# Attention outputs turned by DMA and divided on VectorE, and three smaller edits, in a one-core decoder layer

## The chip, the cores and the metric

One core of a Trainium2 chip runs the whole kernel. The metric is device time in microseconds (us). The kernel before was timed three times: 1709.32 us median, 1707.47 to 1713.86. Engines: PE is TensorE (matmuls and transposes by matmul), PEld its weight loads, DVE is VectorE, ACT is ScalarE, POOL is GpSimd, SP is SyncE, which here only starts DMAs.

## The reference, cut to what matters

Eight batches of 512 queries and 256 dims attend to 1601 context rows, with 16 heads of 16 dims. A self-attention before it touches only 16 rows per batch, and the feed-forward network after it picks one of eight adapters per batch.

```python
x = _layernorm(x + self_attention(x))                    # its result changes 16 rows per batch
q, k, v = split_heads(x @ Wq.T), split_heads(mem @ Wk.T), split_heads(mem @ Wv.T)
scores  = einsum('bhqd,bhkd->bhqk', q, k) / sqrt(16)     # 8 x 16 x 512 x 1601
out     = einsum('bhqk,bhkd->bhqd', softmax(scores), v)
x = _layernorm(x + merge_heads(out) @ Wo.T)
top1 = argmin over the 8 units of mean((decode(encode(x)) - x)**2)
x = _layernorm(x + x @ W_base + b_base + adapter[top1](x))
```

## The kernel before, in words

**Tiling.** Cross-attention is done in 32 groups (8 batches x 4), a group being 4 of the 16 heads. A group is 13 slots, one for each tile of 128 context rows. So a batch is 52 slots (numbered 0 to 51 below) and the kernel 416. In every slot (`pe_slot`) PE makes four score tiles [128 keys x 512 queries], one for each head, from stacked bf16 parts (`pe_scores`). ACT turns each into probabilities (`act_exp`), and PE multiplies those of the slot before with the values (`pe_values`). `values` is one PSUM bank in which each head has 32 partitions: 16 rows of unnormed output and one row of sums of exponentials.

**Maxima.** The exponentials need each query's maximum. Two slots' worth of work ahead, PE makes the scores a second time, queries by keys (`pe_pair`, two double-bank tiles per slot), and DVE reduces each of them (`dve_pair`). In slot 9 of a group DVE joins the pieces and splits the maxima into two bf16 parts (`dve_max_parts`). PE then turns them (job `max`), DVE copies them out of PSUM, ACT's queue writes them to DRAM and reads them back as two more rows of the query stack (`act_max_out`, `act_max_in`), so that the score matmul subtracts them.

**Jobs.** All else goes through one PSUM bank, `work` (`W`): two tables written by hand say which job stands in the middle of a slot (`IN_BETWEEN`) and which at its end (`SLOT_END`). A job has the bank alone; the semaphores `work_full` and `work_free` count through them. A group's output is such a chain: ACT copies `values` to `oS` (`xo_unnormed`) in the next group's first slot (`act_values_out`); job `otr` turns it on PE in four transposes (L932); DVE takes reciprocals of the sums and multiplies into `ox` (L1434, L1435). Once for a batch, jobs `oT` turn `ox` back (2 x 4 transposes, ACT copies each), and jobs `xo` multiply with Wo. DVE's other small work stands in `VECTOR_WORK`, by slot.

**SP's queue.** `sp_batch` is a fixed order of DMA issues, each behind the semaphores that it needs; SP waits at each. `sp_stacks` builds half a batch's stacks: 6 query DMAs, 6 key DMAs, 2 mask DMAs ("top"), then 6 and 6 more ("low").

**PSUM.** `banks` has six banks: two for scores (`SRING`), and two tiles of two for the maxima (`MRING`). The last group has no maxima to make ahead. After it `pe_tail` finishes the last batch.

Of the kernel before, what the change touches and what calls it, by code (L numbers as in the profile page):

```python
# [23 lines left out]
P = 128  # L24
# [6 lines left out]
GH = 4  # L31
# [59 lines left out]
def program(nc, g):  # L91

    with ExitStack() as whole:
# [21 lines left out]
        g.max_dram = nc.dram_tensor("max_dram", (2 * GH * QT, P), BF16, kind="Internal").ap()  # L115

# [29 lines left out]
def short_self_attention(nc, g, s, view, beside):  # L146
# [38 lines left out]
    adiff = sb("s_abs_diff", [TOK, D])  # L185
# [527 lines left out]
def cross_attention_and_ffn(nc, g):  # L713

    sem, W, ident, ident_b, scores, pairs, av = g.sem, g.W, g.ident, g.ident_b, g.scores, g.max_scores, g.av
    Wb = W[:].bitcast(BF16)
    with ExitStack() as s:
# [43 lines left out]
        ox = sb("ox", [P, QT, D])  # L761
# [3 lines left out]
        err = sb("err", [P, 2, T])  # L765
        loss = sb("loss", [P, NPAIR])
# [15 lines left out]
        evac = sem("x_values_out")  # L782
        x1_in = sem("x_x1_in")
# [4 lines left out]
        own = {e: sem(f"x_own_{e}") for e in ("dve", "pool")}  # L788

        def signals(stage):  # L790
# [106 lines left out]
        def work_in_order():  # L897

            for sl in range(B * SLOTS):
                job, part, parts = at_end(sl)  # L900
                for one in (in_between(sl), job if part == 0 else None):
                    if one:
# [10 lines left out]
                         20: ("kproj", 7, 0), 22: ("v", 6, 0), 24: ("qproj", 1, 0), MXG + 1: ("max", 0, 0),  # L913
                         MXG + 2: ("v", 7, 0), MXG + 4: ("v", 0, 0), MXG + 6: ("v", 1, 0)}
# [35 lines left out]
        def pe_job(ph, job, part=0, parts=1):  # L950
# [21 lines left out]
            elif name == "oT":  # L972
                last = transposes(W, ox, i)
# [114 lines left out]
        def pe_next_pair(of, x):  # L1088
# [1201 lines left out]
```

## Time and profile before

| | |
|---|---|
| median of 3 runs | 1709.32 us |
| the profiled execution's own time, as its span | 1708.3 us |
| PE busy | 1623.0 us (95%) |
| DVE busy | 1234.7 us (72%) |
| ACT busy | 1063.1 us (62%) |
| mean granted TensorE clock | 0.991 |
| DMA queue of SP, share of 16 engines' span | 33.7% |

The span runs from the first to the last instruction of the profiled execution. Busy shares are means over stages that differ: the main loop is about 1530 us of it, from the first slot at 122.8 us. A slot's length can be read from the timeline as the distance between two starts of its first pair of score matmuls (L1107).

### The profile page before, as it was taken

Reading aid. Unit: us, or ns where it says so; the run is one execution under the profiler, and the core shown is the slowest. Engines: PE = TensorE matmul, PEld = TensorE weight load, DVE = VectorE, ACT = ScalarE, POOL = GpSimd, SP = SyncE. Lnnn points to the kernel's source line nnn. Section 1 sums busy time; section 2 is a strip of 40 time slices with the busy share of each in tenths; the row PEclk is TensorE's granted clock in tenths of the full one; section 3 lists DMA queues with packets and bytes.
Section 4 is the critical chain, followed back from the end, with each engine's and each line's share of the span. In section 5 each row is a group of like instructions: output and inputs, shape, how many; then the busy total and the mean of one; then the engine's idle time right before and its main releaser. Section 6 shows DMA issues by size and latency. Waiting matters only on the chain.

```text
span 1708.3 us, 25766 instructions
## 1 busy us (share of the span) xinstructions
PE 1623.0 (95%) x9848; PEld 607.9 (36%) x9848; DVE 1234.7 (72%) x1790; ACT 1063.1 (62%) x2012; POOL 160.9 (9%) x151
## 2 busy tenths in 40 slices
PE   6879989999999999999999999999999999999987
PEld 5442323333334333333334333332334323332234
DVE  5687767877778777876778777887778777777423
ACT  2226766676666766676666666676666766666651
POOL 6310000100011000100011000100001000000000
PEclk9889999999999999999999999999999999999999
DMA  5663070604316070624407070523507050420000
GB/s 153 119 154 75 24 137 14 122 29 101 62 47 103 23 133 21 108 56 86 77 24 123 18 136 26 97 67 76 86 1 138 25 85 26 83 30 2 4 25 16
DMA packets 101342, 116.58 MB, mean 68 GB/s; under 512 B 21834, under 2 KB 86987, under 8 KB 101220
## 3 DMA queue, kind: packets, MB, share of 16 engines
q1 hardware_dynamic: 98484, 113.89, 33.7%
q8 instruction: 78, 1.28, 0.4%
q10 hardware_dynamic: 2736, 1.06, 0.3%
q14 instruction: 44, 0.36, 0.1%
HBM read 80.12 MB, written 34.78 MB: 67 GB/s over the span
## 4 chain that ended last, share of the span: by engine, by line
PE 84%; ACT 5%; DVE 5%; issue 4%; DMA 1%; ACTq 0%; SPq 0%; POOL 0%; POOLq 0%; DVEq 0%
PE banks L1107 22%; PE values L1126 22%; PE banks L1081 12%; PE work L990 5%; PE work L1004 5%; ACT xprobs L1256 4%; PE work L947 4%; PE work L1011 3%; PE work L1017 3%; PE work L932 3%; DVE xneg_max_pieces L1444 1%; PE work L1020 1%; PE work L996 1%; PE work L1029 1%; DVE xv_rows L1402 1%
## 5 line engine op out<-in xcount | busy, mean ns | idle before, releaser
L1256 ACT ACTIVATE xprobs<-banks 128x512 f32<-128x512 f32 x1664 | 902.4, 595 | 451.0 <-PE banks L1107 434.7
L1444 DVE TENSOR_REDUCE xneg_max_pieces<-banks 128x2 f32<-128x1024 f32 x768 | 910.3, 1221 | 279.5 <-PE banks L1081 277.3
L1107 PE MATMUL banks<-xq_stacks,xk_stacks 99*128 99x512 bf16 (+1 forms) x1664 | 522.9, 385 | 28.1 <-ACT xprobs L1256 20.3
L1126 PE MATMUL values<-xprobs,xv_rows 128*17 128x512 f32 x3328 | 437.9, 598 | 1.0 <-ACT xprobs L1256 1.0
L1107 PEld LDWEIGHTS banks<-xq_stacks,xk_stacks 99*128 99x128 bf16 (+1 forms) x1664 | 128.1, 97 | 418.7 <-ACT xprobs L1256 278.1
L1081 PE MATMUL banks<-xk_stacks,xq_stacks 49*128 49x512 bf16 (+1 forms) x2048 | 249.3, 336 | 9.1 <-DVE xneg_max_pieces L1444 8.2
L1081 PEld LDWEIGHTS banks<-xk_stacks,xq_stacks 49*128 49x128 bf16 x2048 | 56.5, 94 | 280.1 <-DVE xneg_max_pieces L1444 160.5
L1511 POOL TENSOR_TENSOR xk_parts<-xk_rest,xk_parts 128x401 bf16<-128x401 f32 (+1 forms) x64 | 59.0, 922 | 711.9 <-ACT xk_parts L1217 711.9
L1126 PEld LDWEIGHTS values<-xprobs,xv_rows 128*17 128x17 f32 x3328 | 55.1, 95 | 120.4 <-issue 118.9
L1506 POOL TENSOR_TENSOR xrstd<-xrstd,mhalf 128x4 f32<-128x4 f32 x23 | 23.2, 1010 | 649.6 <-DVE xrstd L1316 649.6
L1004 PE MATMUL work<-xvT,ctxT_a 128*128 128x128 f32 (+1 forms) x416 | 57.1, 282 | 3.1 <-DVE xk_rest L1377 1.9
L1004 PEld LDWEIGHTS work<-xvT,ctxT_a 128*128 128x128 f32 (+1 forms) x416 | 54.0, 193 | 14.7 <-issue 4.9
L1447 DVE TENSOR_REDUCE xneg_max_pieces<-banks 128x8 f32<-128x520 f32 x64 | 44.5, 695 | 18.7 <-PE banks L1081 18.7
L1201 ACT ACTIVATE xk_parts<-work 128x401 bf16<-128x401 f32 (+1 forms) x64 | 32.4, 506 | 40.6 <-PE work L990 40.6
L1004 PEld LDWEIGHTS work<-xvT,ctxT_b 128*128 128x128 f32 (+1 forms) x416 | 53.5, 187 | 11.2 <-ACT hT L1165 3.4
L1011 PE MATMUL work<-x2T,wenc 128*128 128x512 f32 x112 | 57.4, 593 | 0.0
L1017 PE MATMUL work<-x2T,wdecT 128*128 128x512 f32 x112 | 57.2, 591 | 0.0
L1004 PE MATMUL work<-xvT,ctxT_b 128*128 128x128 f32 (+1 forms) x416 | 55.6, 275 | 0.0
L990 PE MATMUL work<-ctxT_a,xkT 128*128 128x400 f32 (+1 forms) x128 | 52.2, 528 | 1.1 <-DVE xq_rest L1391 1.1
L990 PE MATMUL work<-ctxT_b,xkT 128*128 128x400 f32 (+1 forms) x128 | 49.7, 510 | 0.0
L1377 DVE TENSOR_TENSOR xk_rest<-work,xk_parts 128x401 f32<-128x401 f32 (+1 forms) x64 | 36.8, 575 | 16.3 <-issue 8.8
L1217 ACT ACTIVATE xk_parts<-xk_rest 128x401 bf16<-128x401 f32 (+1 forms) x64 | 34.8, 544 | 10.9 <-DVE xk_rest L1377 10.9
(301 smaller groups left out, 1063.9 us busy)
## 6 DMA issues: line engine op xcount, KB each, us to landing
xk_stacks<-key_parts_dram SPq DMA_DIRECT2D x186, 200.1 KB, 11.9
key_parts_dram<-xk_parts SPq DMA_DIRECT2D x144, 100.0 KB, 1.7
xq_stacks<-parts_dram SPq DMA_DIRECT2D x186, 64.0 KB, 8.1
ctxT_a<-in_ctxT SPq DMA_DIRECT2D x4, 1601.0 KB, 7.3
ctxT_b<-in_ctxT SPq DMA_DIRECT2D x4, 1601.0 KB, 7.7
parts_dram<-xq_parts SPq DMA_DIRECT2D x45, 128.0 KB, 1.9
key_parts_dram<-xk_parts SPq DMA_DIRECT2D x48, 100.2 KB, 5.1
xa<-in_x SPq DMA_DIRECT2D x8, 512.0 KB, 13.7
```

The source lines that it names most:

```text
L932: last = nc.tensor.transpose(W[:, q * P:(q + 1) * P], src[:, q, c * P:(c + 1) * P], ident[:])
L947: last = nc.tensor.matmul(W[:, i * D:(i + 1) * D], left, right, start=c == 0, stop=c == steps - 1)
L990: last = pe.matmul(W[:, 0:n], xkT[:, kin, c * P:(c + 1) * P], ctx[b % 2][:, kin, k0:k0 + n], start=kin == 0, stop=kin == CH - 1)
L1004: last = pe.matmul(W[0:rows, (tt - first) * P:(tt - first + 1) * P], ctx[b % 2][:, kin, tt * P:tt * P + rows], xvT[:, kin, c * P:(c + 1) * P],
L1011: last = pe.matmul(W[:], wenc[:, kin, 2 * i:2 * i + 2, :].rearrange("p n h -> p (n h)"), x2T[:, kin, :], start=kin == 0, stop=kin == CH - 1)
L1017: last = pe.matmul(W[:], wdecT[:, kin, i * P:(i + 1) * P], x2T[:, kin, :], start=kin == 0, stop=False)
L1081: last = pe.matmul(pairs[n % MRING][:, par, at:at + w], qst[rows, k, h2, par, q * P:(q + 1) * P], kst[rows, k, h2, par, k0:k0 + w], start= ...
L1107: pe.matmul(scores[n % SRING], kst[0:ROWS[par], k, h2, par, t * P:(t + 1) * P], qst[0:ROWS[par], k, h2, par, :], start=True, stop=True).th ...
L1126: last = pe.matmul(av[32 * j:32 * j + HD + 1, :], vals[:, k, t, gr * GH + j, :], probs[:, sl % 2, j, :], start=t == 0, stop=t == XKT - 1)
L1256: nc.scalar.activation(probs[:, sl % 2, j, :], scores[n % SRING], ACT.Exp).then_inc(exped, 1)
L1444: nc.vector.tensor_reduce(nmp[:, of % 2, j2, :, q, piece], pairs[n % MRING][:, :, :], AX.X, ALU.max, negate=True).then_inc(on["mxr"], 1)
L1511: nc.gpsimd.tensor_tensor(kpart[:, i % KBUF, 2, 0:n], krest[:, i % KBUF, 0:n], kpart[:, i % KBUF, 1, 0:n], ALU.subtract).then_inc(on["klow ...
```

## The change: what it does, and the diff

1. **Outputs.** Jobs `otr` and `oT` are gone. SP moves each group's rows from `oS` with DMAs: four of 16 rows into a new tile `oT` [dims x queries], where `xo` reads them, and one that spreads the four rows of sums over 128 partitions (`sp_move_outputs`). DVE takes the reciprocal of that [128 x 16] (`invert`). SP writes it to DRAM and reads it back, each row to 16 partitions (`sp_spread_inverses`), and DVE multiplies half of `oT` by it (`scale`, [64 x 512]).
2. **Maxima.** Job `max` is gone. DVE turns the parts itself in 32 x 32 blocks, and SP, not ACT, does the two DMA steps (`sp_max_rows`).
3. **Tables.** `xo` now stands in slots 6 to 9, `v` 1 in 4 and 5, `x2T` 0 in 14, and the second normalisation's steps one slot later.
4. **Last group.** Its scores go round all six banks, and its four score matmuls stand together at the front of a slot.
5. **Tail.** The first half of the last `xo` is multiplied ahead; the last group's output is turned and turned back as before, but for half the dims.

```diff
         IN_BETWEEN = {
-            1: ("otr", 3, PREV), 2: ("oT", 0, PREV), 4: ("oT", 1, PREV), 8: ("x1T", 0, NEXT), 10: ("max", 1, NOW),
...
+            8: ("x1T", 0, NEXT), 11: ("x1T", 1, NEXT), 14: ("x2T", 0, PREV), 16: ("x2T", 1, PREV), 18: ("v", 3, NOW),
+            35: ("loss", 0, PREV),
         VECTOR_WORK = {
+            1: [("invert", "o", 3, PREV)], 4: [("scale", "o", 3, PREV), ("aggr", "x1", 0, NEXT)],
+            14: [("invert", "o", 0, NOW)], 18: [("scale", "o", 0, NOW)],
+            27: [("invert", "o", 1, NOW)], 32: [("scale", "o", 1, NOW)],
+            40: [("invert", "o", 2, NOW)], 44: [("scale", "o", 2, NOW)],
...
             elif name == "xo":
                 if part == 0:
-                    pe.wait_ge(on["w_free"], ph.order.after(("oT", 1, b)))
-                last = rows_of(W, x2T, xoT, i, units(part, parts, 2 * CH))
+                    pe.wait_ge(scaled, GROUPS * (b + 1))
+                last = rows_of(W, oT, xoT, i, units(part, parts, 2 * CH))
...
+        def score_bank(n):
+            if n < LAST_SCORE:
+                return scores[n % SRING], SRING
+            place = n - LAST_SCORE
+            before = SRING if place < SRING else LAST_RING if place >= LAST_RING else n + 1
+            return g.banks[:, place % LAST_RING, :], before
...
-            for one in pairs_at(m, t):
-                pe_next_pair(*one)
-            pe_scores(m, t, 2)
-            pe_scores(m, t, 3)
+            final = m == B * GROUPS - 1
+            for j in range(GH if final else GH // 2):
+                pe_scores(m, t, j)
...
+            elif name == "invert":
+                v.wait_ge(moved, N_MOVED * (m + 1))
+                v.reciprocal(rs[:, m % 2, :], rs[:, m % 2, :]).then_inc(inverted, 1)
+            elif name == "scale":
+                v.wait_ge(spread, 16 * (m + 1))
+                v.tensor_tensor(oT[these, k, :], oT[these, k, :], rsb[these, :], ALU.mult).then_inc(scaled, 1)
...
+        def sp_max_rows(of):
+            sp.wait_ge(on["comb_ready"], n)
+            sp.dma_start(g.max_dram.rearrange("r (b c) -> b r c", c=32), mrow[:]).then_inc(on["mrow_out"], 16)
+            sp.wait_ge(on["mrow_out"], 16 * n)
+            for par in range(2):
+                sp.dma_start(qst[row:row + 2, ...], src[par]).then_inc(on["max_in"], 16)
+        def sp_move_outputs(m):
+            sp.wait_ge(evac, m + 1)
+            sp.dma_start(rs[:, m % 2, :], oS[HD::2 * HD, :].rearrange("j (s x) -> j s x", x=GH * T // P)).then_inc(moved, 16)
+            for j in range(GH):
+                sp.dma_start(oT[row:row + HD, k, :], oS[2 * HD * j:2 * HD * j + HD, :]).then_inc(moved, 16)
+        def sp_spread_inverses(m):
+            sp.wait_ge(inverted, m + 1)
+            sp.dma_start(g.rsum_dram[m % 2].rearrange("j (s x) -> (j s) x", x=GH * T // P), rs[:, m % 2, :]).then_inc(rs_out, 16)
+            sp.wait_ge(rs_out, 16 * (m + 1))
+            sp.dma_start(rsb[these, :], g.rsum_dram[m % 2].unsqueeze(1).broadcast_to([GH, HD, T])).then_inc(spread, 16)
...
             for top in (True, False):
                 sp_query_stacks(c, top)
                 sp_key_stacks(b, c, top)
+                if top and between is not None:
+                    sp_spread_inverses(between)
...
         def sp_batch(b):
             if prev >= 0:
+                sp_move_outputs(m - 1)
                 sp_load_x1(prev)
-            sp_stacks(b, 1)
+            sp_stacks(b, 1, m - 1 if prev >= 0 else None)
```

PE from the end of slot 0 into slot 2 of a batch, before (`work<-ident,xo_unnormed` is `otr`, `work<-ident,ox` is `oT`):

```order
L990 MATMUL work<-ctxT_a,xkT 128x401 x2
L1107 MATMUL banks<-xq_stacks,xk_stacks 128x512 x2
L1126 MATMUL values<-xprobs,xv_rows 17x512 x4
L932 MATMUL work<-ident,xo_unnormed 128x128 x4
L1081 MATMUL banks<-xk_stacks,xq_stacks 128x512 x4
L1107 MATMUL banks<-xq_stacks,xk_stacks 128x512 x2
L990 MATMUL work<-ctxT_a,xkT 128x400 x2
L1107 MATMUL banks<-xq_stacks,xk_stacks 128x512 x2
L1126 MATMUL values<-xprobs,xv_rows 17x512 x4
L932 MATMUL work<-ident,ox 128x128 x4
```

The same place now:

```order
L998 MATMUL work<-ctxT_a,xkT 128x401 x2
L1122 MATMUL banks<-xq_stacks,xk_stacks 128x512 x2
L1141 MATMUL values<-xprobs,xv_rows 17x512 x4
L1082 MATMUL banks<-xk_stacks,xq_stacks 128x512 x4
L1122 MATMUL banks<-xq_stacks,xk_stacks 128x512 x2
L998 MATMUL work<-ctxT_a,xkT 128x400 x2
L1122 MATMUL banks<-xq_stacks,xk_stacks 128x512 x2
L1141 MATMUL values<-xprobs,xv_rows 17x512 x4
L1082 MATMUL banks<-xk_stacks,xq_stacks 128x65 x8
```

The transposes between the values and the next pair are gone; the rest stands as it did.

DVE in slots 2 to 6 of a batch, before (two reductions `xneg_max_pieces` to a slot):

```order
L1310 BN_STATS xstats<-xa 128x6 x2
L1444 TENSOR_REDUCE xneg_max_pieces<-banks 128x2 x2
L1402 COPY xv_rows<-work 128x32x16
L1310 BN_STATS xstats<-xa 128x6 x2
L1444 TENSOR_REDUCE xneg_max_pieces<-banks 128x2 x2
L1314 BN_AGGR xmeanvar<-xstats 128x2 x4
L1316 TENSOR_SCALAR xrstd<-xmeanvar 128x4
L1444 TENSOR_REDUCE xneg_max_pieces<-banks 128x2 x2
L1396 TENSOR_TENSOR x<-work,x 128x512
L1320 TENSOR_SCALAR xa<-xa,xmeanvar,xrstd 128x256 x2
```

The same place now:

```order
L1301 BN_STATS xstats<-xa 128x6 x2
L1432 TENSOR_REDUCE xneg_max_pieces<-banks 128x2 x2
L1403 COPY xv_rows<-work 128x32x16
L1301 BN_STATS xstats<-xa 128x6 x2
L1432 TENSOR_REDUCE xneg_max_pieces<-banks 128x2 x2
L1324 TENSOR_TENSOR xo_by_dims<-xo_by_dims,err 64x512
L1305 BN_AGGR xmeanvar<-xstats 128x2 x4
L1307 TENSOR_SCALAR xrstd<-xmeanvar 128x4
L1432 TENSOR_REDUCE xneg_max_pieces<-banks 128x2 x2
L1403 COPY xv_rows<-work 128x32x16
L1311 TENSOR_SCALAR xa<-xa,xmeanvar,xrstd 128x256 x2
```

L1324, `scale` of the previous batch's last group, now stands at the end of slot 4, ahead of the statistics and of slot 5's two reductions; it waits for the semaphore of the spread inverses.

SP at the start of a batch, now (`err` is the tile that the inverses are spread over):

```order
L1621 DMA xrsum<-xo_unnormed 128x1x16
L1624 DMA xo_by_dims<-xo_unnormed 16x512 x4
L1658 DMA x<-x_dram 128x4x256
L1589 DMA xq_stacks<-parts_dram 16x4x512 x6
L1576 DMA xk_stacks<-key_parts_dram 16x4x1601 x6
L1581 DMA xk_stacks<-mask_dram 1x4x1664 x2
L1633 DMA rsum_dram<-xrsum 128x16
L1637 DMA err<-rsum_dram 64x1x512
```

Before, SP went from the load of `x` to the stacks, top and low, with nothing ahead of the load and nothing between the masks and the low stacks.

## Rows read from the trace of the kernel before

**Rows 1.** Page: busy us (share) x instructions, by engine.

```profile
PE 1623.0 (95%) x9848; PEld 607.9 (36%) x9848; DVE 1234.7 (72%) x1790; ACT 1063.1 (62%) x2012; POOL 160.9 (9%) x151
```

**Rows 2.** Page: chain that ended last, share of the span by engine.

```profile
PE 84%; ACT 5%; DVE 5%; issue 4%; DMA 1%; ACTq 0%; SPq 0%; POOL 0%; POOLq 0%; DVEq 0%
```

**Rows 3.** Groups by form: count, busy us, mean ns, idle before and releasers.

```profile
L932 PE MATMUL work<-ident,xo_unnormed 128*128 128x128 f32 x128 | 21.0, 286 | 0.8 <-ACT xo_unnormed L1249 0.8
...
L932 PE MATMUL work<-ident,ox 128*128 128x128 f32 x60 | 9.8, 286 | 1.0 <-DVE ox L2139 0.8 <-DVE xk_rest L1377 0.2
...
L1032 PE MATMUL work<-ident_b,xneg_max_parts 128*32 128x128 bf16 x32 | 7.3, 228 | 6.0 <-DVE xv_rows L1402 3.6 <-DVE xneg_max_parts L1470 2.4
```

**Rows 4.** Timeline, PE: start us, us, engine, line; slots 1 to 5, batch 3.

```profile
703.34 0.60 PE L1107 MATMUL banks<-xq_stacks,xk_stacks 99*128 99x512 bf16 x2
...
707.77 0.60 PE L1107 MATMUL banks<-xq_stacks,xk_stacks 99*128 99x512 bf16 x2
...
711.91 0.62 PE L1107 MATMUL banks<-xq_stacks,xk_stacks 99*128 99x512 bf16 x2
...
715.32 0.62 PE L1107 MATMUL banks<-xq_stacks,xk_stacks 99*128 99x512 bf16 x2
...
719.33 0.65 PE L1107 MATMUL banks<-xq_stacks,xk_stacks 99*128 99x512 bf16 x2
```

**Rows 5.** Timeline, PE: last slot of batch 3 and first of batch 4.

```profile
889.87 0.65 PE L1107 MATMUL banks<-xq_stacks,xk_stacks 99*128 99x512 bf16 x2
...
893.66 0.79 PE L1107 MATMUL banks<-xq_stacks,xk_stacks 99*128 99x512 bf16 x2 [0.26 <-ACT xprobs L1256]
```

**Rows 6.** Timeline, last group: ACT in a slot without a job.

```profile
1648.97 2.22 ACT L1256 ACTIVATE xprobs<-banks 128x512 f32<-128x512 f32 x4 [0.65 <-PE banks L1107]
```

**Rows 7.** Timeline, last group, PE: two slots with job y.

```profile
1631.51 0.60 PE L1107 MATMUL banks<-xq_stacks,xk_stacks 99*128 99x512 bf16 x2
...
1634.77 0.60 PE L1107 MATMUL banks<-xq_stacks,xk_stacks 99*128 99x512 bf16 x2
```

**Rows 8.** Timeline, PE: the last batch's xo, after the last group.

```profile
1661.11 1.97 PE L947 MATMUL work<-xoT,x2T 128*128 128x256 f32 x8 [0.88 <-DVE x2T L2142]
```

**Rows 9.** Timeline at a batch's start: ACT, SP's issues.

```profile
701.14 0.60 ACT L1249 ACTIVATE xo_unnormed<-values 128x512 f32<-128x512 f32 x1 [0.28 <-PE values L1126]
...
702.03 2.67 SPq L1597 DMA_DIRECT2D xq_stacks<-parts_dram  x6
...
710.19 3.03 SPq L1597 DMA_DIRECT2D xq_stacks<-parts_dram  x6
```

**Rows 10.** DMA issues from 710.1 to 713.2: KB each, us to landing.

```profile
xq_stacks<-parts_dram SPq DMA_DIRECT2D x6, 64.0 KB, 7.9
```

**Rows 11.** DMA issues from 716.1 to 720: KB each, us to landing.

```profile
key_parts_dram<-xk_parts SPq DMA_DIRECT2D x3, 100.2 KB, 12.7
```

**Rows 12.** DMA issues from 742 to 760: KB each, us to landing.

```profile
key_parts_dram<-xk_parts SPq DMA_DIRECT2D x6, 100.0 KB, 1.7
```

**Rows 13.** Windows: busy by engine, PEclk, DMA share, GB/s.

```profile
707.00:716.00 9.00, 8.80 (x67) 4.02 (x69) 6.71 (x9) 6.56 (x13) 0.95 (x1) 1.00 1.03 139
...
722.00:726.00 4.00, 4.00 (x25) 1.82 (x24) 4.00 (x7) 2.76 (x6) 0.00 (x0) 1.00 1.08 139
```

**Rows 14.** Page: DMA issues over the span, KB each, us to landing.

```profile
wdown<-in_Wdown SPq DMA_DIRECT2D x8, 64.0 KB, 2.0
```

**Rows 15.** Timeline, slots 5 and 6: DVE's reductions, PE's pairs.

```profile
721.32 2.36 DVE L1444 TENSOR_REDUCE xneg_max_pieces<-banks 128x2 f32<-128x1024 f32 x2 [0.56 <-PE banks L1081]
...
724.30 0.61 PE L1081 MATMUL banks<-xk_stacks,xq_stacks 49*128 49x512 bf16 x4
```

**Rows 16.** Groups by form, DVE: reductions of 1024; a product of two tiles in SBUF.

```profile
L1444 DVE TENSOR_REDUCE xneg_max_pieces<-banks 128x2 f32<-128x1024 f32 x768 | 910.3, 1221 | 279.5 <-PE banks L1081 277.3
...
L677 DVE TENSOR_TENSOR xo_unnormed<-xo_unnormed,s_query_roots 128x512 f32<-128x512 f32 x3 | 3.3, 1109 | 0.1
```

**Rows 17.** Windows in the front: busy by engine, PEclk.

```profile
122.40:125.80 3.40, 2.09 (x12) 0.59 (x9) 3.00 (x7) 1.62 (x3) 0.00 (x0) 1.00 1.04 125
125.80:129.30 3.50, 3.50 (x7) 1.31 (x6) 2.30 (x2) 1.64 (x4) 0.00 (x0) 0.51 1.09 129
```

More of the change, by code:

```diff
@@ L1246, in act_values_out @@
             if m:
-                b, i = divmod(m - 1, GROUPS)
-                nc.scalar.wait_ge(on["w_full"], MAIN.order.after(("otr", i, b)))
+                nc.scalar.wait_ge(moved, N_MOVED * m)
             nc.scalar.activation(oS[:], av[:], ACT.Copy).then_inc(evac, 1)
@@ L1484, in dve_slot @@
             if parts:
-                dve_max_parts(MAIN, m + 1, 1)
-                dve_max_parts(MAIN, m + 1, 2)
+                for step in range(1, 4):
+                    dve_max_parts(MAIN, m + 1, step)
             if todo:
@@ L1994, in dve_front @@
                 if n == MXG:
-                    for step in range(3):
+                    for step in range(4):
                         dve_max_parts(FIRST, 0, step)
-                    dve_job(FIRST, ("max", 0, 0))
                 elif n - 1 in BETWEEN_TILES and n < MXG:
@@ L2034, in cross_attention_and_ffn @@
         tail_w = (g.W[:], g.banks[:, 4, :])
+        tail_oT = (g.banks[:, 4, :], g.banks[:, 5, :])
+        tail_xo = [g.banks[:, q, 0:D] for q in range(QT)]
+        ox = rsb.rearrange("p (q n) -> p q n", q=QT)
         tail_enc = [g.banks[:, i, :] for i in range(NPAIR)]
@@ L2043, in pe_tail, with xo @@
             pe.wait_ge(loop["w_free"], len(MAIN.order.names))
+            def xo(c, first, last):
+                for q in range(first, last):
+                    one = pe.matmul(tail_xo[q], oT[:, c, q * P:(q + 1) * P], xoT[:, c, :], start=c == 0, stop=c == CH - 1)
+                return one
+            pe.wait_ge(scaled, B * GROUPS - 1)
+            xo(0, 0, 2)
             pe.wait_ge(evac, B * GROUPS)
             transposes(g.W[:], oS[:].rearrange("p (q n) -> p q n", q=QT), 0).then_inc(t_otr_made, 1)
+            xo(0, 2, QT)
             pe.wait_ge(t_ox_in, 1)
-            for c in range(CH):
-                transposes(tail_w[c], ox, c).then_inc(t_oT_made, 1)
-            for one in t_oT_in:
+            for q in range(QT):
+                one = pe.transpose(tail_oT[q // 2][:, q % 2 * P:(q % 2 + 1) * P], ox[:, q, :], ident[:])
+                if q % 2:
+                    one.then_inc(t_oT_made, 1)
+            for i, one in enumerate(t_oT_in):
                 pe.wait_ge(one, 1)
-            for i in range(2):
-                rows_of(tail_w[i], x2T, xoT, i, range(2 * CH)).then_inc(t_xo_made, 1)
+                xo(1, 2 * i, 2 * i + 2).then_inc(t_xo_made, 1)
             pe_keep_busy(pe, KEEP_NORM, g.banks[:, 5, :])
```

202 lines of the change are left out of this document (109 added, 93 removed).

## The prediction, made before the changed kernel ran

> **What bounds the kernel now.** I read the busy shares first, then the chain that ended last: PE is busy for 95% of the span and makes 84% of the chain [rows 1, 2]. So what counts is how much PE time the change takes away, and whether another engine or a wait then ends the slots. The groups by form give the work that goes: 128 transposes of `xo_unnormed` and 60 of `ox`, 21.0 and 9.8 us busy, and 32 of the maxima, 7.3 us [rows 3]. The timeline gives what such a job is worth, because slots repeat: a slot with a `v` part alone takes 711.91 to 715.32, 3.41 us; the same with `oT` in its middle takes 715.32 to 719.33, 4.01 us; the slot with `otr` and a key projection takes 703.34 to 707.77, 4.43 us [rows 4].
>
> The sum is made against the profiled execution's span, 1708.3 us, which lies 1.0 us under the median of the runs.
>
> **What goes.** *Transposes of outputs:* an `oT` costs 4.01 - 3.41 = 0.60 us, and an `otr` is the same four transposes (21.0 / 32 = 0.66 us busy against 9.8 / 15 = 0.65), so 0.6 us too. The main loop has 31 `otr` and 14 `oT`: 45 x 0.6 = 27.0 us. *Turning the maxima on PE:* 7.3 us busy and 6.0 us of idle PE before them over 32, 0.42 us each [rows 3]; 31 of them give 0.4 x 31 = 12.4 us, against 7.3 if the idle time stays. That VectorE does the turn instead costs it a small instruction in place of a copy from PSUM; I take nothing. *ACT's DMA issues:* a batch's last slot takes 889.87 to 893.66, 3.79 us, although only a short job stands in it [rows 5]; ACT issues the two reads of the maxima there. Without them 3.41, so 0.38 x 7 = 2.7 us. *Last group:* in a slot without a job ACT works 2.22 us and sits idle 0.65 us for the next scores [rows 6]. With six banks and four scores ahead the idle time goes, since PE's own work there (four scores, eight value matmuls) is under 2.1 us. In the four `y` slots (3.26 us each, [rows 7]) PE is itself the bound, so nothing. Seven slots and one with `otr` beside `mid`: 8 x 0.6 = 4.8 us. *Tail:* four of eight transposes (0.65 us, rows 3's price) leave the path; the first half of `xo` took 1.97 us [rows 8] and has half of its matmuls behind it beforehand, 1.0; and smaller copies 0.3: 2.0 us. Together 27.0 + 12.4 + 2.7 + 4.8 + 2.0 = 48.9 us.
>
> **What comes: a wait at the start of seven batches.** SP now works through a longer list. The outputs are ready when ACT's copy ends, 701.14 + 0.60 = 701.74 [rows 9]. Then come five moves and the load of `x`, at 2.67 / 6 = 0.45 us an issue (the six query issues of rows 9): 2.7 us, so the first stack DMA starts at 704.5, not 702.03. The top stacks (14 issues) took from 702.03 to 710.19 [rows 9], 8.2 us, and now end at 712.7. Only then is the write of the inverses issued, and here is the price: it stands in SP's DMA queue behind 1.6 MB of stacks. The rows show what that means. Queries' low stacks issued at 710.19 landed 7.9 us later, about 718.1, although they are 64 KB each [rows 10]; the key parts issued behind the low stacks took 12.7 us, where the same DMA takes 1.7 us in a quiet queue [rows 11, 12]. In between the DMA engines were busy throughout (share 1.03, 139 GB/s, [rows 13]). So the top stacks are through at about 717.7 (0.4 us less, which 64 KB take at that rate), with the late start 720.2, and the write lands then, not at 714.5. SP waits for it, then issues the spread (128 KB from DRAM to 64 partitions). The nearest rows are 64 KB from DRAM in 2.0 us [rows 14] as a lower end, and 128 KB more at 139 GB/s of 16 engines spread over fewer of them as an upper, up to 5 us; I take 2.6, near the former, since the queue is then empty. The inverses are there at 722.8.
>
> The Trainium skill, page "DMA: Bandwidth & Descriptors", section "Queues, rings and completion order", says that on each DMA engine descriptors are consumed in ring order, and that a copy runs on the largest k of up to 16 engines that divides both sides' slowest dimension; the first half the trace agrees with (12.7 against 1.7 us), the second no row here shows for this shape. By it the spread, whose source has four rows, would run on four engines; that is the rival of the slow spread below.
>
> DVE's `scale` stands at the end of slot 4. With slot 1 at 3.8 and slots 2 to 4 at 3.41 us, slot 5 starts at 717.4. DVE ends a slot's reductions 0.94 us into the next (721.32 + 2.36 = 723.68 against slot 6's start, 719.33 + 3.41 = 722.74 [rows 4, 15]), so it gets to `scale` at 718.3 and waits 4.5 us. Then come `scale` itself, for which the rows give 0.61 us (half of a 1024-column pass of 1.22) to 1.11 us [rows 16], taken as 0.7, and the statistics, 0.6, both ahead of slot 5's two reductions (2.4 us): done at 722.8 + 0.7 + 0.6 + 2.4 = 726.5. PE wants the pair banks for slot 6 at 1.56 us into the slot (724.30 - 722.74 [rows 15]), the second at 1.9, which is now 717.4 + 3.4 + 1.9 = 722.7. So PE stands 3.8 us, in each of batches 1 to 7: 26.6 us. Ends: 1 us (7 in all) if the write overtakes part of the stacks; 6.5 us (45) if the spread needs 5 us.
>
> The wait also holds slot 5's `v` copy and through it `xo`; these are late by the same 3.8 us, not in addition. DVE has no slack to make it good: it is busy 4.00 of 4.00 us there [rows 13]. By my count slots 2 to 9 of a batch now ask 28.1 us of it against 27.8 of PE; another 0.3 x 7 = 2 us.
>
> The other uses of the same DMAs I cost at nothing. Groups 0 and 2 have a short queue: moves in the slot of `evac`, `invert` at the end of the next, inverses about 5 us later, `scale` four slots on (13.6 us). Group 1 has the top stacks ahead too, but six slots: by the same sum the inverses are there about 22 us after slot 26's start, `scale` at 24. Maxima are ready in slot 9 of a group and wanted 4 slots (14 us) later, for two DMAs of some 2 us. If that cover is gone, each of 24 groups pays what it is late.
>
> Sum: 1708.3 - 48.9 + 26.6 + 2.0 = 1688.0 us. I forecast **1688**, its own range 1678 to 1699.
>
> **Rivals.**
> - *No wait at the batch start* (the inverses land early): 1708.3 - 48.9 + 2 = 1661. Against it: rows 11; for it: only that this write is 8 KB. 11%.
> - *The clock falls in the stall.* PE would stand nearly 4 us at once in a loop in which it never did. In the front, 2.09 us busy of 3.40 was followed by a stretch at 0.51 of full clock, 1.2 GHz [rows 17]. A fall for one such stretch of 3.5 us costs half of it, 1.75 x 7 = 12 us: 1700; two stretches 1712. Against it: DVE is late then, and hides a part. 20%, about 1700.
> - *Slow spread.* 128 KB over four engines, a quarter of 139 GB/s, takes 3.7 us and not 0.9: 2.5 us x 7 = 17 more, 1705. 9%.
> - *DVE takes over as the bound* in the slots freed: it is at 72% on average but full in stretches; half of the 39.4 us of removed PE jobs would be lost, 1708. 7%.
> - *Slower:* the moves and the two-step trip through DRAM are late in every group, not only the seven. A move reads and writes only 16 partitions; if the five land 1.2 us after DVE comes to `invert`, DVE, PE and SP wait in all of the other 24 groups: 24 x 1.2 = 29 us, 1717, and slower beyond that. At 1.5 us: 1724. Against it: four slots of room and quiet queues in those places. 7%.
> - My forecast: 46%.
>
> **How the numbers follow.** What a measurement of this kernel can tell from no change is 0.5%, 8.5 us, so faster is under 1700.8 and slower over 1717.9. Faster: all of the first rival, nearly all of the forecast, half of the clock, a third of the slow spread: 0.11 + 0.44 + 0.10 + 0.03, with a little of the fourth 0.69. Slower: the last rival and a tail of the clock, 0.08. Same: 0.23. The range reaches from the first rival to the slow spread and the fourth, 1662 to 1708.
>
> **What would show it.** Right: slots 2 to 4 of a batch at 3.41 us; slot 10 near 3.9; DVE idle some 4 us before `scale` in slot 4 with the spread as releaser, and no such idle time in slots 18, 32 and 44; the write of the inverses landing 7 us after issue in seven places and under 2 in the others; the last group's plain slots at 2.2 us. Wrong: no idle time before `scale` (the first rival), a granted clock under 0.99 in the loop (the second), idle time before `invert` or in all `scale` (the last), or freed slots still over 3.41 us while DVE is full (the fourth).

## The result, and the profile after

| | before | changed |
|---|---|---|
| median of 4 runs each, us | 1711.09 (1707.47 to 1713.86) | 1728.01 (1724.41 to 1730.19) |
| profiled span, us | 1708.3 | 1726.6 |
| mean granted clock | 0.991 | 0.973 |

The ratio is 1.0106, 95% interval 1.0091 to 1.0121: slower by 1%, where I forecast 1688 us and 1662 to 1708. The page's busy line and chain, against [rows 1, 2]:

```profile
PE 1602.8 (93%) x9632; PEld 591.3 (34%) x9632; DVE 1239.7 (72%) x1790; ACT 1053.8 (61%) x1998; POOL 161.5 (9%) x151
...
PE 74%; DMA 8%; DVE 5%; SPq 5%; ACT 4%; issue 4%; POOL 0%; POOLq 0%; DVEq 0%; ACTq 0%
```

PE does 20.2 us less work in a span 18.3 us longer. The chain, which was 84% PE, now has 8% DMA and 5% SP's queue in it. The waits name the place (us in total, times, longest), DVE's first and PE's second:

```profile
DVE xo_by_dims L1324 <- DMA err<-rsum_dram: 71.3, 14, 9.9
```

```profile
PE banks L1082 <- DVE xneg_max_pieces L1432: 63.5, 28, 7.8
```

`err<-rsum_dram` is the spread of the inverses (`rsb` is a part of `err`), L1324 is `scale`. The same batch start as in [rows 4, 9], in the timeline of SP's queue (start us, us, instruction):

```profile
703.20 0.63 SPq L1621 DMA_DIRECT2D xrsum<-xo_unnormed  x1
703.87 2.48 SPq L1624 DMA_DIRECT2D xo_by_dims<-xo_unnormed  x4
706.44 0.53 SPq L1658 DMA_DIRECT2D x<-x_dram  x1
707.20 2.69 SPq L1589 DMA_DIRECT2D xq_stacks<-parts_dram  x6
...
713.15 1.30 SPq L1581 DMA_DIRECT2D xk_stacks<-mask_dram  x2
714.56 0.37 SPq L1633 DMA_DIRECT2D rsum_dram<-xrsum  x1
722.57 0.58 SPq L1637 DMA_DIRECT2D err<-rsum_dram  x1
723.20 2.79 SPq L1589 DMA_DIRECT2D xq_stacks<-parts_dram  x6
```

DVE and PE in the timeline of the same stretch:

```profile
717.41 2.34 DVE L1432 TENSOR_REDUCE xneg_max_pieces<-banks 128x2 f32<-128x1024 f32 x2
727.47 0.69 DVE L1324 TENSOR_TENSOR xo_by_dims<-xo_by_dims,err 64x512 f32<-64x512 f32 x1 [7.72 <-DMA err<-rsum_dram]
```

```profile
718.73 0.62 PE L1122 MATMUL banks<-xq_stacks,xk_stacks 99*128 99x512 bf16 x2
...
722.14 0.62 PE L1122 MATMUL banks<-xq_stacks,xk_stacks 99*128 99x512 bf16 x2
...
729.96 0.61 PE L1082 MATMUL banks<-xk_stacks,xq_stacks 49*128 49x512 bf16 x2 [6.21 <-DVE xneg_max_pieces L1432]
731.09 0.60 PE L1082 MATMUL banks<-xk_stacks,xq_stacks 49*128 49x512 bf16 x2 [0.52 <-DVE xneg_max_pieces L1432]
...
734.16 1.06 PE L1122 MATMUL banks<-xq_stacks,xk_stacks 99*128 99x512 bf16 x2
...
738.19 0.65 PE L1122 MATMUL banks<-xq_stacks,xk_stacks 99*128 99x512 bf16 x2
```

The chain reads downwards: SP issues the write at 714.56, gets past its wait at 722.57 (8.0 us), issues the spread, and DVE, which had been ready since 719.75, starts `scale` at 727.47. PE fills slot 6 up to its pairs and stands 6.21 us. Batch 3 is the mildest of the seven: over all of them the write takes 8.0 to 9.6 us and DVE waits 7.7 to 9.9. Slots 6 and 7 last 722.14 to 738.19, 16.05 us; undisturbed (in experiment 1 below) they take 6.79, so this batch start loses 9.3 us. Over the seven, slots 6 and 7 lose 69.1 us. The two score matmuls that start slot 7 take 1.06 us in place of 0.6; the windows (busy by engine, PEclk, DMA share, GB/s) say why:

```profile
721.30:728.80 7.50, 2.44 (x19) 1.06 (x17) 1.26 (x7) 2.10 (x4) 0.00 (x0) 1.00 0.51 108
728.80:735.60 6.80, 5.12 (x16) 2.15 (x20) 6.38 (x9) 1.79 (x4) 1.01 (x1) 0.50 1.04 129
735.60:739.00 3.40, 3.40 (x24) 1.31 (x20) 2.23 (x2) 1.80 (x4) 0.00 (x0) 1.00 1.06 236
```

After a stretch with 2.44 us of PE work in 7.5, the granted clock is 0.50, 1.2 GHz, for 6.8 us. It falls so in all seven batch starts, twice for 6.8 and five times for 10.2 us.

The slots that were to get shorter did: from slot to slot of batches 1 to 6, slot 1 went from 4.43 to 3.84 us, slot 4 from 4.00 to 3.41, slot 10 from 4.35 to 3.91, slot 27 from 4.00 to 3.41, slot 51 from 3.78 to 3.27. In a plain slot of the last group ACT's row [rows 6] became:

```profile
1649.80 2.06 ACT L1253 ACTIVATE xprobs<-banks 128x512 f32<-128x512 f32 x4 [0.57 <-PE banks L1122]
```

(this one is behind a `mid` job; the four plain slots after it take 1.96 us each, against 2.87.)

### The profile page after: what moved, and what is told of

Its sections match the earlier page's. It is cut to its first block, busy times and chain, and to the rows that moved or that the text cites. A ratio compares the mean times of both kernels' runs of the same rounds, so it can differ in the third digit from the quotient of the medians.

```text
span 1726.6 us, 25559 instructions
## 1 busy us (share of the span) xinstructions
PE 1602.8 (93%) x9632; PEld 591.3 (34%) x9632; DVE 1239.7 (72%) x1790; ACT 1053.8 (61%) x1998; POOL 161.5 (9%) x151
## 4 chain that ended last, share of the span: by engine, by line
PE 74%; DMA 8%; DVE 5%; SPq 5%; ACT 4%; issue 4%; POOL 0%; POOLq 0%; DVEq 0%; ACTq 0%
PE banks L1122 20%; PE values L1141 20%; PE banks L1082 11%; DMA rsum_dram<-xrsum 5%; PE work L1012 4%; PE work L957 4%; PE work L998 4%; ACT xprobs L1253 3%; DVE xneg_max_pieces L1432 3%; DMA err<-rsum_dram 3%; PE work L1019 3%; PE work L1025 2%; SPq L1589 2%; PE work L1004 2%; SPq L1576 1%
## 5 line engine op out<-in xcount | busy, mean ns | idle before, releaser
L1082 PE MATMUL banks<-xk_stacks,xq_stacks 49*128 49x512 bf16 (+1 forms) x2048 | 254.3, 339 | 65.5 <-DVE xneg_max_pieces L1432 63.5
L1324 DVE TENSOR_TENSOR xo_by_dims<-xo_by_dims,err 64x512 f32<-64x512 f32 x31 | 21.1, 681 | 71.3 <-DMA err<-rsum_dram 71.3
L1012 PEld LDWEIGHTS work<-xvT,ctxT_a 128*128 128x128 f32 (+1 forms) x416 | 54.3, 192 | 13.7 <-issue 3.9
```

Of the source, the lines that this page charges most:

```text
L1012: last = pe.matmul(W[0:rows, (tt - first) * P:(tt - first + 1) * P], ctx[b % 2][:, kin, tt * P:tt * P + rows], xvT[:, kin, c * P:(c + 1) * P],
L1082: last = pe.matmul(pairs[n % MRING][:, par, at:at + w], qst[rows, k, h2, par, q * P:(q + 1) * P], kst[rows, k, h2, par, k0:k0 + w], start= ...
```

## The experiments

Ratios are to the kernel before, timed on the same chip, with 95% intervals. "Stall" is what slots 6 and 7 of batches 1 to 7 take over 6.79 us.

### 1. The spread ahead of the stacks

```diff
-                sp_load_x1(prev)
-            sp_stacks(b, 1, m - 1 if prev >= 0 else None)
+                sp_load_x1(prev)
+                sp_spread_inverses(m - 1)
+            sp_stacks(b, 1)
```

> At a batch's start SP writes and spreads the previous group's inverses before it issues the stacks, not between the top and the low ones. Theory 1 (the write stands in SP's DMA queue behind the top stacks; the wait of DVE for the spread is the whole loss): the write lands in about 2 us, the spread in 3 to 5, DVE does not wait at its scale in slot 4, slots 6 and 7 of batches 1 to 7 take 3.41 us each and not 12.5 and 4.1; 9.7 x 7 = 68 us less than the changed kernel, 1659 us, clock 0.99. Theory 2 (the late stacks only move the wait: SP now waits for the reciprocal in slot 1 before it issues any stack, some 4 us later than in the changed kernel): pairs or scores wait for stacks, 1665 to 1690. Theory 3 (the loss is DVE's, which is full in slots 2 to 9): still over 1700.

Measured: 1662.63 us (1660.86 to 1664.36), ratio 0.9711 [0.9675, 0.9747], span 1662.5. The stall is nil in all seven: PE's slots 6 and 7 of batch 3 start at

```profile
706.50 0.62 PE L1122 MATMUL banks<-xq_stacks,xk_stacks 99*128 99x512 bf16 x2
...
709.89 0.65 PE L1122 MATMUL banks<-xq_stacks,xk_stacks 99*128 99x512 bf16 x2
```

and in the view of DMA issues from 688 to 697 us (KB each, us to landing) the same write takes

```profile
rsum_dram<-xrsum SPq DMA_DIRECT2D x1, 8.0 KB, 2.1
```

In the other six starts it takes 1.4 us five times and 1.9 once. So two issues moved ahead of fourteen in SP's row are worth 65 us. What remains of DVE's waits for the spread is

```profile
DVE xo_by_dims L1324 <- DMA err<-rsum_dram: 16.5, 7, 3.1
```

and all seven stand at the start of slot 33 of batches 0 to 6: group 1's write is also issued behind top stacks. I had said that slot 32's `scale` would not wait.

### 2. Write and spread from ACT's queue

```diff
-            sp_stacks(b, 1, m - 1 if prev >= 0 else None)
+            sp_stacks(b, 1)
...
+            if m and m % GROUPS == 0 and t == 2:
+                act_inverses_out(m - 1)      # wait for inverted; the write
+            if m and m % GROUPS == 0 and t == 3:
+                act_inverses_in(m - 1)       # wait for the write; the spread
```

> The seven late groups' inverses are written and spread from ACT's DMA queue, at the ends of slots 2 and 3; SP's stacks stay where they were and run at the same time. Theory 1 (what holds the write is the order in its own queue, not the load of the 16 DMA engines): it lands in 2 to 3 us although the stacks run, the spread in 3 to 5, DVE waits under 1 us; 1660 us. Theory 2 (the engines are full, whichever queue it comes by): the write lands some 8 us after its issue at the end of slot 2, the spread is issued after slot 5 and DVE waits 8 us or more; 1727 us or slower.

Measured: 1777.54 us (1763.8 to 1778.22), ratio 1.0359 [1.0304, 1.0414]. Timeline, ACT's queue and DVE, batch 3:

```profile
728.85 0.32 ACTq L1252 DMA_DIRECT2D rsum_dram<-xrsum  x1
...
736.26 0.53 ACTq L1259 DMA_DIRECT2D err<-rsum_dram  x1
```

```profile
751.80 0.69 DVE L1341 TENSOR_TENSOR xo_by_dims<-xo_by_dims,err 64x512 f32<-64x512 f32 x1 [14.48 <-DMA err<-rsum_dram]
```

From a queue in which nothing stands ahead, the write still needs 7.4 us while SP's stacks are in flight (5.7 to 8.5 over the seven starts), and the spread, now issued among the low stacks, 15.5 us. So a queue of their own does not free these small DMAs from the stacks that SP has issued before them. ACT also waits itself (20.5 us in 5 times), and PE with it. The Trainium skill, page "DMA: Bandwidth & Descriptors", section "Issuing engines are not separate DMA queues", says that the DMAs of all issuing engines run on the same 16 DMA engines and interleave there; this trace agrees, with 7.4 us against 8.0 on SP's own queue.

### 3. No wait and no division

```diff
-                v.wait_ge(spread, 16 * (m + 1))
-                v.tensor_tensor(oT[these, k, :], oT[these, k, :], rsb[these, :], ALU.mult)
+                v.tensor_tensor(oT[these, k, :], oT[these, k, :], oT[these, k, :], ALU.mult)
...
-            if m >= 2:
-                sp.wait_ge(scaled, m - 1)
+            if m:
+                sp.wait_ge(spread, 16 * m)
```

This kernel leaves out the division: DVE still makes a pass of the same size, but squares the outputs, and SP waits for the previous spread where it had waited for `scaled`.

> All DMAs and the reciprocals stay as in the changed kernel, but DVE's scale squares the outputs in place and does not wait for the spread inverses, so the softmax isn't divided. Theory 1 (only DVE's wait for the spread costs): 68 us less than the changed kernel, 1659 us, clock 0.99, and slots 6 and 7 at 3.41 us. Theory 2 (the DMA traffic itself, or SP being held for 8 us behind the write, costs elsewhere): over 1670.

Measured: 1658.77 us (1656.52 to 1660.75), ratio 0.9693 [0.9657, 0.9729], span 1656.2, no stall, and slot 34 at 3.75 us in batches 1 to 6, where the first experiment has up to 5.1. The spans 1708.3 and 1656.2 make the gain of everything but the waits 52.1 us; against the changed kernel's 1726.6, the waits for the spread, with the clock that falls behind them, cost 70.4 us.

### 4. The scale one slot later

```diff
-            4: [("scale", "o", 3, PREV), ("aggr", "x1", 0, NEXT)],
+            4: [("aggr", "x1", 0, NEXT)],
...
-            5: norm_steps("apply", "x1", 0, 2, NEXT),
+            5: norm_steps("apply", "x1", 0, 2, NEXT) + [("scale", "o", 3, PREV)],
```

> DVE's scale of the previous batch's last group stands at the end of slot 5, not 4; the DMAs are as in the changed kernel. DVE then comes to it 3.4 us later plus the 0.7 us of the step put ahead. Theory 1 (wait, then clock): DVE waits 7.7 - 4.1 = 3.6 us, PE stands about 3 us instead of 6.8; 7 x 3.9 = 27 us less, 1700 us, with the clock still falling; if such a stall is too short for the clock to fall, another 7 x 2.2 less, 1685 us. Theory 3 (DVE's work, not its wait, is the loss): no change, 1727 us.

Measured once: 1704.58 us, span 1702.8. DVE's waits for the spread come to

```profile
DVE xo_by_dims L1324 <- DMA err<-rsum_dram: 40.5, 14, 4.5
```

The stall falls from 69.1 to 42.1 us, the 27 us of theory 1. In the seven starts DVE waits only 25.4 us, though, so here a stall is longer than the wait by more than half. PE's timeline in batch 3 shows another path than before: `xo` waits for `scale` itself.

```profile
722.79 1.24 PE L957 MATMUL work<-xoT,xo_by_dims 128*128 128x256 f32 x4 [3.46 <-DVE xo_by_dims L1324]
```

These idle times of PE are 3.3 to 4.1 us, 26.9 us in the seven starts. The other 15 us are the clock, which still falls each time, for 3.4 us in five and 6.8 in two (window of batch 3, slot 6):

```profile
723.62:727.03 3.41, 3.41 (x14) 0.44 (x13) 2.15 (x4) 1.08 (x2) 0.00 (x0) 0.50 1.06 132
```

PE is busy for all of this window and loses half of it: beyond PE's idle time, a fall of 3.4 us costs 1.8 here and one of 6.8 us 3.0 to 3.1. Each of these idle times, about as long as the 3.8 us of stall that I had forecast, was followed by a fall.

### 5. TensorE kept busy in the stall

```diff
+                if j == 1 and m and m % GROUPS == 0 and t == 6:
+                    nn = GH * sl + j
+                    nc.tensor.wait_ge(exped, nn - score_bank(nn)[1] + 1)
+                    for _ in range(24):
+                        nc.tensor.matmul(score_bank(nn)[0], ident_b[:], ident_b[:].unsqueeze(1).broadcast_to([P, 4, P]),
+                                         start=True, stop=True)
                 pe_scores(m, t, j)
```

> In slot 6 of batches 1 to 7 TensorE first does 24 matmuls of the identity (some 5.1 us at 0.214 us each), whose result is overwritten, in place of most of the 6.2 us in which it stood there. DVE's wait for the inverses is as before. Theory A, the fall of the clock is a part of the 9.7 us that a batch start lost (the stretches at half clock after the stall cost about 2.9 us of it): the granted clock stays at 1.00 there, slot 6 is near 9.7 and slot 7 at 3.4 us, the wait of scale for the spread stays near 71 us in total, and the time is 1728 - 7 x 2.9 = about 1708 us. Rival B, the half clock is hidden behind DVE, which is late anyway: slots 6 and 7 together stay near 16.5 us and the time is 1728 us within 5, full clock or not.

Measured: 1718.94 us (1716.1 to 1725.91), ratio 1.0068 [1.0047, 1.009], span 1714.3. The clock fell in four of the seven (3.4 us each) and not in batches 1, 4 and 5, which gives the comparison inside one run. Batch 4, no fall, DVE and PE:

```profile
918.05 0.69 DVE L1330 TENSOR_TENSOR xo_by_dims<-xo_by_dims,err 64x512 f32<-64x512 f32 x1 [7.21 <-DMA err<-rsum_dram]
```

```profile
913.23 0.38 PE L1122 MATMUL banks<-xq_stacks,xk_stacks 99*128 99x512 bf16 x1
913.46 5.35 PE L1156 MATMUL banks<-ident_b 128*128 128x512 bf16 x24
...
923.30 0.65 PE L1122 MATMUL banks<-xq_stacks,xk_stacks 99*128 99x512 bf16 x2
...
926.80 0.38 PE L1122 MATMUL banks<-xq_stacks,xk_stacks 99*128 99x512 bf16 x1
```

Its stall is 926.80 - 913.23 - 6.79 = 6.78 us for a wait of 7.21, 0.43 less; batches 1 and 5 give 0.44 and 0.43 less too. Batch 3, with the fall, loses 8.83 us for a wait of 7.77, which is 1.49 over that rule (0.9 to 1.5 in the four batches with a fall):

```profile
725.90:729.30 3.40, 3.40 (x14) 1.11 (x12) 3.12 (x5) 1.95 (x4) 0.00 (x0) 0.50 1.05 131
```

So with `scale` in slot 4 and full clock a stall is the wait less 0.43 us, and what is over that is the clock. In the changed kernel the seven waits are 58.9 us; by this rule, an estimate, 58.9 - 7 x 0.43 = 55.8 of the 69.1 us are the wait, and 13.3 us, 1.9 a batch, are the clock. I had expected 2.9 a batch and 1708 us. Neither theory's total came, since four falls remained; that the clock costs something, and how much, stands on these batches.

### 6. The low stacks wait for the spread

```diff
                     sp_spread_inverses(between)
+                    nc.sync.wait_ge(spread, 16 * (between + 1))
```

> SP waits until the spread of the inverses has landed before it issues the low stacks, at the seven batch starts. Theory A, the spread takes 4.9 us from issue to landing because the low stacks are issued right behind it and share its DMA engines: alone it lands some 2.6 us after issue, slot 6 loses 2.3 us and the clock's fall gets shorter, so 16 to 25 us less than the changed kernel: 1703 to 1712 us. Rival B, the spread is slow by its own shape (four source rows, 64 written): it still lands 4.5 to 5 us after issue and the time stays at 1728 us within 5.

Measured: 1718.46 us (1715.44 to 1721.32), ratio 1.0054 [1.0035, 1.0072]. Timeline, SP's queue and DVE:

```profile
720.44 0.58 SPq L1637 DMA_DIRECT2D err<-rsum_dram  x1
```

```profile
723.96 0.69 DVE L1324 TENSOR_TENSOR xo_by_dims<-xo_by_dims,err 64x512 f32<-64x512 f32 x1 [7.16 <-DMA err<-rsum_dram]
```

Alone the spread takes 3.5 us, not 4.9 and not 2.6 (means of the seven starts: 3.6 against 4.9): both theories have a share. The stall falls from 69.1 to 55.3 us. Two windows of the stretch in which its data moves:

```profile
722.00:722.50 0.50, 0.00 (x0) 0.00 (x0) 0.00 (x0) 0.00 (x0) 0.00 (x0) 1.00 0.23 90
722.50:723.00 0.50, 0.00 (x0) 0.00 (x0) 0.00 (x0) 0.00 (x0) 0.00 (x0) 1.00 0.26 102
```

The DMA share is 0.00 in the 1.5 us before its data moves, so nothing else is in flight, and then 0.23 to 0.26: as much as four busy engines of sixteen. At 90 to 102 GB/s the 128 KB are moved in some 1.5 us, and some 1.4 us pass between the issue and the first of them. Four engines are thus faster than the quarter of 139 GB/s by which I had priced them.

### 7. The spread as four DMAs

```diff
-                v.wait_ge(spread, 16 * (m + 1))
+                v.wait_ge(spread, 64 * (m + 1))
...
-            sp.dma_start(rsb[these, :], g.rsum_dram[m % 2].unsqueeze(1).broadcast_to([GH, HD, T])).then_inc(spread, 16)
+            for j in range(GH):
+                row = these.start + j * HD
+                sp.dma_start(rsb[row:row + HD, :],
+                             g.rsum_dram[m % 2, j:j + 1].broadcast_to([HD, T])).then_inc(spread, 16)
```

> The spread is issued as four DMAs, one for each head (one source row to 16 partitions). Theory A, low stacks behind it are what makes it slow: the four issues cost SP 1.4 us more at 0.45 us each, so DVE waits 1 to 1.4 us longer in each batch start and the time is 1728 + 7 to 10 = 1735 to 1738 us. Rival B, the one DMA with four source rows is served by few DMA engines: the last of four lands under 3.5 us after the first issue, DVE waits 1.5 us less or more and the time is 1710 to 1720 us.

Measured: 1710.02 us (1704.69 to 1715.67), ratio 1.0002 [0.9986, 1.0019], span 1713.9. Timeline:

```profile
722.31 1.71 SPq L1639 DMA_DIRECT2D err<-rsum_dram  x4
```

```profile
725.43 0.69 DVE L1324 TENSOR_TENSOR xo_by_dims<-xo_by_dims,err 64x512 f32<-64x512 f32 x1 [5.89 <-DMA err<-rsum_dram]
```

All four have landed 3.1 us after the first issue begins, 1.8 sooner than the one DMA of the same bytes, though they cost SP 1.1 us more. Each of them lands 1.7 to 2.1 us after its own issue, against 3.5 for the one DMA alone, so its shape has a share in the slow spread. How large a share stays open: the low stacks are issued behind the four as well, but 1.8 us after the first of them and not 0.6, so this run moves the stacks too. The Trainium skill, page "DMA: Bandwidth & Descriptors", section "Rules for kernel authors", says that an outermost dimension smaller than 16 confines a DMA to at most that many engines; with four source rows the share of 0.23 to 0.26 in experiment 6 agrees.

### 8 and 9. The last group's banks alone, the maxima alone

The kernel before with `score_bank` and the last group's order of scores, and nothing else:

> The kernel before with the last group's scores on six banks, four issued ahead, and nothing else changed. My forecast was 8 slots x 0.6 = 4.8 us. The changed kernel's last group shows plain slots of 1.96 us against 2.87, which by eight such slots, with 0.1 us more in each of four y slots, would be about 7 us: 1704 us against 1711. Rival: the last group's slots shrink in the changed kernel because the otr transposes and copies are gone too; then this alone gives under 3 us, 1708 or more.

Measured: 1704.39 us (1702.22 to 1706.18) against 1709.84, ratio 0.9966 [0.9954, 0.9979]: 5.5 to 5.8 us. The plain slots are the changed kernel's 1.96 us, so the banks alone do it; the rival falls.

The kernel before with `sp_max_rows` and DVE's turn of the maxima, and nothing else:

> The kernel before with the rows of maxima turned by DVE and moved by SP, and nothing else of the change: 31 transposes of maxima leave TensorE's row and the three DMA issues for each group leave ACT's. My sum gave 12.4 us for the transposes with the idle time before them and 2.7 us for ACT's issues in the last slot of a batch: 15 us less, about 1695 against 1710. Rival: the slots that had such a transpose are held by ACT or DVE as well, so that only the 7.3 us of busy time or less goes: 1702 or more. If the reads of maxima wait behind SP's key parts, TensorE waits for them at a group's start and the time is 1710 or above.

Measured: 1692.56 us (1690.97 to 1694.82) against 1709.2, ratio 0.9899 [0.9882, 0.9915]: 17 us, with an interval of 14.5 to 20 that holds the 15 of the forecast. In the profiled executions the loop's slots are shorter by 15.1 us in all. The last slot of batch 3, 3.79 us before [rows 5], in PE's timeline:

```profile
881.12 0.65 PE L1106 MATMUL banks<-xq_stacks,xk_stacks 99*128 99x512 bf16 x2
...
884.39 0.79 PE L1106 MATMUL banks<-xq_stacks,xk_stacks 99*128 99x512 bf16 x2
```

is 3.27, under a plain slot's 3.41, where I had taken 3.41.

### 10. The first experiment, and group 1's scale in slot 33

```diff
-            27: [("invert", "o", 1, NOW)], 32: [("scale", "o", 1, NOW)],
+            27: [("invert", "o", 1, NOW)], 33: [("scale", "o", 1, NOW)],
```

> The changed kernel with the spread before the stacks at the batch starts (as in the first experiment) and group 1's scale one slot later, at the end of slot 33. In the first experiment DVE stood 1.5 to 3.1 us for the spread only there, in slot 33 of batches 0 to 6, because SP issues that write behind the top stacks too. Theory: this wait is what the first experiment still loses against the kernel without any wait (1662.6 against 1658.8 us): slot 34 goes back to 3.75 us, no wait for the spread over 1 us is left in the loop, and the time is 1657 to 1660 us. Rival: those 4 us are the division and its place on DVE (31 passes of 675 ns) or SP's longer row, and then it stays at 1662 us or rises, since slots 33 to 35 are full on DVE.

Measured: 1658.2 us (1656.54 to 1659.29), ratio 0.9704 [0.969, 0.9717], span 1654.8. No wait of DVE for the spread is left in the loop, and slot 34 is at 3.75 us in batches 1 to 6. The page:

```profile
PE 1584.6 (96%) x9632; PEld 588.7 (36%) x9632; DVE 1239.8 (75%) x1790; ACT 1053.3 (64%) x1998; POOL 161.0 (10%) x151
...
PE 88%; DVE 4%; ACT 4%; issue 3%; POOL 1%; DMA 0%; SPq 0%; POOLq 0%; DVEq 0%; ACTq 0%
```

This version beats both kernels: 51 us, 3%, under the one before. The medians put it 4.4 us under the first experiment, but the two were timed on different chips and the ratios' intervals overlap; that the move of `scale` gains stands on slot 34 only. It has the division and is as fast as the kernel of experiment 3, so once the inverses come in time the division adds nothing that can be seen. What the passes of `scale` and SP's longer row cost by themselves is not shown by that, since both kernels have them. PE's busy time gives a measure of the clock: the changed kernel's 1602.8 us, for the same 9632 matmuls, are 18.2 more than here, where the clock falls nowhere in the loop.

## Why the prediction was wrong

- **What goes: right, a little small.** I had 48.9 us, less 2.0 for a fuller DVE: 46.9. Experiment 3's span gives 52.1. By slot lengths, its loop before the last group is 42.8 us shorter; with experiment 9's 15.1 for the maxima (15.1 forecast) that leaves 27.7 for the outputs (27.0). The last group gives 5.4 (4.8), what follows it 2.7 (2.0), and the part ahead of the first slot 1.1; that part's length differs from run to run (118.2 to 124.5 us). The 2.0 for a fuller DVE did not show: slots 5 and 9 stay at 3.41 us and slots 18 and 44, which hold a `scale`, at 3.99 and 3.80, as before.
- **The wait at the batch starts: right in place, cause and count, wrong in size. This is the step that failed**, with the clock put at nothing in the sum (below). I priced it 3.8 x 7 = 26.6 us; slots 6 and 7 lost 69.1. Slot 1 of batch 3 starts 1.43 us later than in [rows 4]; with that added, my times for the batch against the trace's:

| step, batch 3 | forecast | trace |
|---|---|---|
| first stack issued | 705.9 | 707.20 |
| write issued | 714.1 | 714.56 |
| write landed | 721.6 | 722.55 |
| DVE ready for `scale` | 719.7 | 719.75 |
| spread landed | 724.2 | 727.4 |
| DVE's wait | 4.5 | 7.72 |

  The first stack came 1.3 us late: the five moves took 0.62 us of SP each and not 0.45, and the rest went to the load of `x` and the gaps between the issues. The top stacks' issues made up 0.8 of it; 0.5 more went to the landing. The spread's 2.6 us, the value taken near the lower end of "up to 5", was 4.9: that is the larger error. On the mean of the seven the wait was 8.4 us, since the write took up to 9.6 us elsewhere; by experiment 5's rule that is 55.8 us of stall, 29.2 more than forecast. My upper end for a spread of 5 us, written as 6.5 us and 45 in all, comes to 6.2 and 43 by its own terms, so even that end lies below what the waits cost.
- **The clock.** The sum had nothing for it. I held it apart as a rival of 12 us or more; it came on top of the wait, 13.3 us. It did not need the longer wait: in experiment 4 PE stood 3.3 to 4.1 us, about the 3.8 that I had forecast, and the clock fell all seven times. So the forecast's own stall should have been priced with the fall. The slow spread, too, was a rival priced alone, at 17 us (3.7 - 0.9 is 2.8 us and not 2.5, so 20). Both rivals were true at once. The range ended where one of them alone would have gone.
- **Groups at nothing:** right for groups 0 and 2. Group 1's `scale` did wait, 1 to 3 us in seven batches, 12.4 us in all, of which PE lost 2.4. Its write is issued behind top stacks as well; I had counted 22 us after slot 26's start for its inverses and 24 for `scale`. DVE came to `scale` at 24.7 us, but the inverses at 25.7 to 27.7.
- **The mechanism of the queue: not shown.** I wrote that the write stands in SP's queue behind 1.6 MB. Experiment 2 shows that the same write from another queue, beside the same stacks, gains only 0.6 us in batch 3. The 12.7 against 1.7 us of [rows 11, 12], which I took as agreeing with ring order, thus do not tell the queue from the load on the DMA engines; the price for SP's queue came out near, 8.0 us for 7.5.

In sum: 1688.0 - 5.2 (more gained) + 29.2 (wait) + 13.3 (clock) + 2.4 (group 1) = 1727.7, against a span of 1726.6.

These corrections were read from the same runs that they explain, so the sum is a check of the account and not a proof of it. What shows the cause is that the first experiment's order makes the wait vanish, and that experiment 10 then lies at 1658 us, near what I had for "no wait" (1661).

On the write, the windows of the changed kernel (busy by engine, PEclk, DMA share, GB/s) say that the stacks' data is nearly through at 721:

```profile
719.00:720.00 1.00, 1.00 (x10) 0.19 (x9) 0.75 (x1) 0.79 (x2) 0.00 (x0) 1.00 0.96 132
720.00:721.00 1.00, 1.00 (x9) 0.23 (x6) 0.00 (x0) 0.30 (x1) 0.00 (x0) 1.00 0.64 58
721.00:722.00 1.00, 1.00 (x9) 0.94 (x8) 0.00 (x0) 0.77 (x2) 0.00 (x0) 1.00 0.08 11
```

The write landed at 722.55, some 1.5 us later, about the 1.4 us that it takes undisturbed. That fits a write which moves only once the stacks' data is through, but no run separates the two parts. Not settled either: how the spread's 4.9 us divide between its shape and the low stacks behind it.

## What to carry to other kernels

A small DMA whose result an in-order engine waits for belongs ahead of bulk transfers in the issue order; another queue did not do instead here. Before writing down a landing time, ask what is in flight then, and how few rows the DMA's outermost dimension has. When a stall is forecast on the bounding engine, price the clock's fall as a part of it, not as an alternative, and combine rivals that can be true together before drawing the range. An edit that is right in the sum but late at one place deserves another order of issues before it is given up: here that turned 17 us lost into 51 gained.

## What the runs showed of the hardware that I had not expected

- A DMA with four rows outermost kept the DMA share at 0.23 to 0.26 with nothing else in flight, moved 90 to 102 GB/s, and took 3.5 us for 128 KB, of which some 1.4 passed before its data moved; four DMAs to 16 rows each, one after the other, took 3.1 (experiments 6 and 7).
- An 8 KB write took 1.4 to 2.1 us ahead of the stacks, 8.0 to 9.6 behind them in the same queue, and 5.7 to 8.5 beside them in another.
- Moves of 16 partitions from SBUF to SBUF cost SP 0.62 us of issue each (2.48 for four), where the query stacks' DMAs from DRAM cost 0.45.
- Behind idle times of TensorE of 2.5 to 9.4 us at the batch starts the granted clock was 0.50 for 3.4, 6.8, 10.2 or 13.7 us. Where the engine had been kept busy with 24 matmuls in the stall, it did not fall in three of seven places and fell for 3.4 us in the other four.
- What a fall costs depends on what else is late: one of 6.8 us cost 3.0 to 3.1 us in experiment 4, where TensorE had work for 6.0 to 6.2 us of it, and 1.2 to 2.8 us by experiment 5's rule where VectorE was late as well.
